# Expert layer 2 of a mixture-of-experts block as seven half-size products, with the experts written out

## The chip, the cores and the metric

One Trainium2 chip, one of its cores. The metric is the device time of one execution in microseconds; lower is better. All data are float32 (some small tables of the first stage are bfloat16).

## The reference, cut to what matters

The program is a block of three layers over 4 images of 32x32 tokens of 384 channels: a selective scan with a depthwise convolution, a linear attention, and a mixture of experts. Only the last is touched:

```python
B, S, D = x.shape                                # 4, 1024, 384
E = router_w.shape[1]                            # 8 experts
T = B * S                                        # 4096 tokens
C = T // E                                       # 512 slots for each expert
...
expert_inputs = jnp.einsum('td,tec->ecd', xf, dispatch)
h = gelu(jnp.einsum('ecd,edm->ecm', expert_inputs, w1) + b1[:, None, :])
expert_outputs = gelu(jnp.einsum('ecm,emd->ecd', h, w2) + b2[:, None, :])
out = jnp.einsum('ecd,tec->td', expert_outputs, combine)
```

For each of the 8 experts, layer 1 takes 512 slots x 384 to 512 x 1536, and layer 2 takes that back to 512 x 384. The gated result is added to the token rows.

## The kernel before

Each engine runs a stream of its own, written by hand, and the streams meet in semaphores. The stages follow each other: the scan (to about 1410 us), its output projection, the attention with the routing (to about 1720 us), and then the experts (to the end).

Before the experts, each token's row has been stored to slot_in in DRAM by its slot, and the token rows to tok_dram and out. An expert e then goes like this; its buffers go by its parity, s.

SyncE (lines 543 to 558) loads w1[s], w2[s] (2.3 MB each) and the slot rows xe. After the first two experts, the loads for e + 2 wait for og_ok, the last gelu of expert e, and all go out together.

TensorE (`turn_slots` from 1474, `expert` from 1481) does three things.
- It transposes xe with 12 instructions into PSUM banks 0 to 2 (line 1478). This is done for e + 1 in the middle of layer 2 of e (TURN_AT = 1, after token tile 1).
- Layer 1 (line 1489): 12 groups m of 128 hidden channels, each of three products (k = 128 channels) over 512 slots, in PSUM banks 3 to 5. From the fourth group on it waits for the gelu of the group three before.
- Layer 2 (line 1502): 4 tiles of 128 slots, each of 12 products over 384 output channels, with the hidden values h_sb as weights and w2 as the moving operand, in banks 6 and 7. It waits for hg_ok of the last gelus at the first tile, and for ob_ok (bank read) at the others.

Each product of float32 operands is two matmul records in the profile, each with a weight load. The program's order on each engine is fixed.

ScalarE (from line 1028) copies the transposed slots to xeT (1032), does the gelu of layer 1 from PSUM to h_sb (1041), and the gelu of layer 2 (1048). VectorE (`owners`, then `expert`) adds the bias b2 to layer 2's PSUM bank into y_pre (2066), and multiplies the gelu by the gate and adds the residual rows (2071). GpSimd (`residuals` 661, `rows_out` 668) gathers residual rows and scatters output rows with indirect DMAs, one of each for a tile of 128 slots; the output rows of e come before the residual rows of e + 1.

Experts 0 to 5 are three turns of a loop over two experts on SyncE, TensorE and VectorE; ScalarE loops over experts 2 to 5. The last two are written out.

Lines of other stages that the prediction reads: 1399 (the attention's 128x128 products, one after the other), 1361 (the transposes behind them), 604 and 587 (GpSimd's products in the scan), 627 and 637 (GpSimd's sums in the two stages after it), 1631, 1856, 1921 and 1963 (VectorE's sums with both inputs in SBUF), 1688 (VectorE's product with an input in PSUM), 531 (the store of token rows to out), 537 (the load of w2[0]).

Of the kernel before, what the change touches and what calls it, by code (L numbers as in the profile page):

```python
# [16 lines left out]
P = 128  # L17
# [39 lines left out]
TURN_AT = 1  # L57
# [101 lines left out]
def hybrid_block_kernel(nc, a, out):  # L159
    with ExitStack() as ctx:  # L160
        def sem(name):
            return ctx.enter_context(nc.semaphore(name))
# [114 lines left out]
        b2_bc = r6y.take(E, C)  # L277
        r6 = Region(arena, R4 + CT * M, COLS)
        w2[0] = r6.take(MT, C)
        xe, xeT, h_sb = r6.take(CPT, CW), r6.take(2, CT, CAP), r6.take(MT, CAP)  # L280
        y_pre, yo, res = r6.take(2, C), r6.take(CPT, C), r6.take(CPT, C)
# [28 lines left out]
        def attend_bank(i):  # L310
            return 4 + (i + 2) % 4


# [3 lines left out]
        token_ok = sem("token_numbers")  # L317
# [5 lines left out]
        cpe_ok, slot_out = sem("conv_filled"), sem("conv_out_of_slot")  # L323
# [30 lines left out]
        tln_ok, x2c_ok, x2_ok = sem("token_var_log"), sem("x2_centred"), sem("x2_ready")  # L354
# [4 lines left out]
            "slots_turned", "slots_turned_copied", "h_filled", "h_gelu", "o_filled", "o_biased", "o_gelu", "rows_scattered"))  # L359
        meta_ok, res_ld, fin_ok = sem("slot_owner"), sem("residuals_in"), sem("final_ready")  # L360
# [19 lines left out]
        def _(sp):  # L380
# [155 lines left out]
            sp.dma_start(xe, slot_in_v[0]).then_inc(ld_xe, 16)  # L536
            sp.dma_start(w2[0], w2_v[0]).then_inc(ld_w2[0], 16)
# [24 lines left out]
        def _(pool):  # L562
# [4 lines left out]
            nc.gpsimd.iota(token, [[P, NT]], base=0, channel_multiplier=1).then_inc(token_ok, 1)  # L567
# [114 lines left out]
        def _(act):  # L682
# [282 lines left out]
            def last_token_std(g):  # L965
                half = slice(4 * g, 4 * g + 4)
                act.wait_ge(tvar_ok, NP + (B - 1) * 2 + (g + 1))
                nc.scalar.activation(rstd5[:, half, 0], mv5[:, half, 1], ACT.Ln, bias=eps_col).then_inc(tln_ok, 1)
                act.wait_ge(tln_ok, g + 1)
                nc.scalar.activation(rstd5[:, half, 0], rstd5[:, half, 0], ACT.Exp, scale=-0.5).then_inc(tstd_ok, 1)  # L970
# [63 lines left out]
            def expert(e, s, first, last):  # L1034
                for m in range(MT):
                    act.wait_ge(h_ok, e * MT + (m + 1))
                    if m == 0:

                        act.wait_ge(o_ok, e * CPT + 2)
                    settled(act)  # L1040
                    nc.scalar.activation(h_sb[:, m], ps[:, 3 + m % 3, :], ACT.Gelu_apprx_tanh,  # L1041
                                         bias=b1_col[:, e, m:m + 1]).then_inc(hg_ok, 1)

                if not first:
                    act.wait_ge(yo_st, e * (16 * CPT))
                for i in range(CPT):
                    act.wait_ge(ob_ok, 1 + e * CPT + (i + 1))
                    nc.scalar.activation(yo[:, i], y_pre[:, i % 2], ACT.Gelu_apprx_tanh).then_inc(og_ok, 1)  # L1048
                    if i == TURN_AT and not last:
                        slots_turned(e + 1, 1 - s)  # L1050

            slots_turned(0, 0)
            expert(0, 0, True, False)
            expert(1, 1, False, False)
            with nc.scalar.Fori(1, E // 2 - 1) as g:
                for s in range(2):
                    expert(g * 2 + s, s, False, False)
            expert(E - 2, 0, False, False)
            expert(E - 1, 1, False, True)
# [3 lines left out]
        def _(pe):  # L1063

            pe.sem_inc(ya_ok, HRING)
            for s in (tp_ok, gr_ok, o_ok):
                pe.sem_inc(s, 2)
# [413 lines left out]
            def expert(e, s, loads, last):  # L1481
                pe.wait_ge(ld_w1[s], loads)
                for m in range(MT):
                    if m >= 3:
                        pe.wait_ge(hg_ok, e * MT + (m - 2))
                    for t in range(CT):
                        if m == 0:
                            pe.wait_ge(xtc_ok, e * CT + (t + 1))
                        mm = pe.matmul(ps[:, 3 + m % 3, :], w1[s][:, t, m * P:(m + 1) * P], xeT[:, s, t],  # L1489
                                       start=(t == 0), stop=(t == CT - 1))  # L1490
                    mm.then_inc(h_ok, 1)
                pe.wait_ge(ld_w2[s], loads)
                for i in range(CPT):
                    if i >= 2:
                        pe.wait_ge(ob_ok, 1 + e * CPT + (i - 1))
                    else:
                        pe.wait_ge(ob_ok, 1 + e * CPT)
                    for m in range(MT):
# [6 lines left out]
                    if i == TURN_AT and not last:  # L1505
                        turn_slots(e + 1)

            turn_slots(0)
            with nc.tensor.Fori(0, E // 2 - 1) as g:
                for s in range(2):  # L1510
                    expert(g * 2 + s, s, g * 16 + 16, False)
            expert(E - 2, 0, 8 * E, False)
            expert(E - 1, 1, 8 * E, True)


        @block.vector
        def _(dve):
# [460 lines left out]
            dve.wait_ge(token_ok, 1)  # L1978
# [79 lines left out]
            def expert(e, s, last):  # L2058
                for i in range(CPT):
                    dve.wait_ge(o_ok, e * CPT + (i + 3))  # L2060

                    if i >= 2:
                        dve.wait_ge(og_ok, 1 + e * CPT + (i - 1))
                    else:
                        dve.wait_ge(og_ok, 1 + e * CPT)
                    nc.vector.tensor_tensor(y_pre[:, i % 2], ps[:, 6 + i % 2, 0:C],  # L2066
                                            b2_bc[:, e, :], ALU.add).then_inc(ob_ok, 1)
                    dve.wait_ge(og_ok, 1 + e * CPT + (i + 1))
                    dve.wait_ge(meta_ok, e + 1)
                    dve.wait_ge(res_ld, e * (16 * CPT) + 16 * CPT)  # L2070
                    nc.vector.scalar_tensor_tensor(out=yo[:, i], in0=yo[:, i], scalar=g_slot[:, s, i:i + 1], in1=res[:, i],  # L2071
                                                   op0=ALU.mult, op1=ALU.add).then_inc(fin_ok, 1)
                    if i == TURN_AT and not last:
                        owners(e + 1, 1 - s)
# [3 lines left out]
            with nc.vector.Fori(0, E // 2 - 1) as g:  # L2078
                for s in range(2):
                    expert(g * 2 + s, s, False)  # L2080
            expert(E - 2, 0, False)
            expert(E - 1, 1, True)


# [79 lines left out]
```

## Time and profile before

| | us |
|---|---|
| median of three runs | 2246.8 (2243.82 to 2249.24) |
| span of the profiled execution | 2244.7 |
| TensorE busy | 1984.1 (88%) |
| VectorE busy | 1575.2 (70%) |
| GpSimd busy | 1297.0 (58%) |
| ScalarE busy | 1144.9 (51%) |

The page gives no time beside the profiled execution's span; the span runs from its first to its last instruction. In the page's slices each digit stands for 1/40 of the span (56.1 us) and is the busy share in tenths. In the chain of waits each piece has its start, its length and what ran. In groups of instructions the columns are line, engine, operation, shapes and count, then busy time and mean ns of one, then idle time before them and what ended it. PE is TensorE, PEld its weight loads, DVE VectorE, ACT ScalarE, POOL GpSimd, SPq the queue that SyncE issues to.

### The profile page before, as it was taken

The numbers are of one execution on the slowest core, as the hardware profiler recorded it, in microseconds if no ns is written. First come the engines' busy times: TensorE is split into PE (matmuls) and PEld (weight loads), VectorE is DVE, ScalarE is ACT, GpSimd is POOL, SyncE is SP. The second block draws the span as 40 slices with busy tenths as digits, with TensorE's granted clock in tenths as the row PEclk, the third lists the DMA queues.
The fourth block names the chain that finished last, engine by engine and source line by source line (L and its number), as shares of the span: only waits on it lengthen the run. The fifth ranks groups of instructions, "written<-read, shape, count | busy, mean of one in ns | idle before, by whom it ended". The sixth has DMA issues, their size and how long they took to land.

```text
span 2244.7 us, 20167 instructions
## 1 busy us (share of the span) xinstructions
PE 1984.1 (88%) x5826; PEld 919.6 (41%) x5830; DVE 1575.2 (70%) x1505; ACT 1144.9 (51%) x1258; POOL 1297.0 (58%) x464
## 2 busy tenths in 40 slices
PE   7988588888888888888888888989995999999997
PEld 3332133333333333333333333456653555555554
DVE  6978999999999999999999999774553000000000
ACT  4788666666776676776767666211213112122111
POOL 0110499999999999999999999401233011111110
PEclk9987599999999999999999999999997999999999
DMA  6448622233222233222232220611226233333300
GB/s 193 151 175 280 212 75 75 70 98 79 84 66 65 75 100 91 65 75 75 61 105 67 77 73 19 229 42 57 85 85 223 85 119 124 123 119 126 126 24 7
DMA packets 82402, 229.13 MB, mean 102 GB/s; under 512 B 14031, under 2 KB 40257, under 8 KB 80816
## 3 DMA queue, kind: packets, MB, share of 16 engines
q1 hardware_dynamic: 76208, 211.54, 29.6%
q0 software_dynamic: 6144, 16.98, 2.1%
q8 instruction: 24, 0.39, 0.1%
q14 instruction: 26, 0.21, 0.0%
HBM read 166.39 MB, written 64.03 MB: 103 GB/s over the span
## 4 chain that ended last, share of the span: by engine, by line
PE 46%; DVE 23%; issue 17%; POOL 8%; ACT 3%; DMA 1%; DVEq 0%; SPq 0%; ACTq 0%; POOLq 0%
DVE arena L1705 15%; PE ps L1489 11%; PE ps L1502 11%; PE ps L1229 6%; POOL arena L604 4%; POOL arena L587 4%; PE ps L1439 3%; PE ps L1213 2%; PE ps L1110 2%; DVE ps L1688 1%; PE ps L1226 1%; PE ps L1139 1%; PE ps L1390 1%; PE ps L1428 1%; DVE arena L1572 1%
## 5 line engine op out<-in xcount | busy, mean ns | idle before, releaser
L604 POOL TENSOR_TENSOR arena<-arena 128x2048 f32<-128x2048 f32 x192 | 868.3, 4533 | 16.6 <-DVE arena L1705 15.7
L1229 PE MATMUL ps<-arena 128*128 128x512 f32 x1536 | 727.7, 596 | 27.7 <-POOL arena L604 27.6
L1705 DVE TENSOR_TENSOR_SCAN arena<-arena,ps 128x1024 f32<-128x1024 f32 x264 | 587.5, 2266 | 0.0
L880 ACT ACTIVATE arena<-ps 128x1024 f32<-128x1024 f32 x384 | 390.7, 1017 | 248.0 <-PE ps L1213 246.1
L1213 PE MATMUL ps<-arena 96*128 (+1 forms) x1296 | 366.7, 384 | 129.3 <-DVE arena L1705 112.7
L1229 PEld LDWEIGHTS ps<-arena 128*128 128x128 f32 x1536 | 288.4, 190 | 287.7 <-issue 194.0
L587 POOL TENSOR_TENSOR arena<-arena 128x1024 f32<-128x1024 f32 x120 | 283.1, 2359 | 103.5 <-DMA arena<-b_rows 103.5
L2066 DVE TENSOR_TENSOR arena<-ps,arena 128x384 f32<-128x384 f32 x32 | 17.8, 557 | 450.4 <-PE ps L1502 450.4
L1688 DVE TENSOR_TENSOR ps<-ps,arena 128x1024 f32<-128x1024 f32 x264 | 309.1, 1216 | 12.6 <-PE ps L1213 12.6
L873 ACT ACTIVATE arena<-arena 128x1024 f32<-128x1024 f32 x264 | 300.8, 1139 | 8.9 <-DVE arena L1705 8.3
L1213 PEld LDWEIGHTS ps<-arena 96*128 96x128 bf16 x1296 | 112.9, 98 | 461.3 <-DVE arena L1705 215.7
L668 POOL DMA_INDIRECT out<-arena x32 | 31.7, 992 | 437.4 <-DVE arena L2071 437.4
L1705 DVE TENSOR_TENSOR_SCAN arena<-ps,arena 128x1024 f32<-128x1024 f32 x120 | 271.5, 2262 | 4.6 <-ACT ps L873 4.2
L1489 PE MATMUL ps<-arena 128*128 128x512 f32 x576 | 250.2, 595 | 0.0
L1502 PE MATMUL ps<-arena 128*128 128x384 f32 x768 | 250.2, 486 | 0.0
L1502 PEld LDWEIGHTS ps<-arena 128*128 128x128 f32 x768 | 145.4, 190 | 101.5 <-issue 3.8
L873 ACT ACTIVATE ps<-arena 128x1024 f32<-128x1024 f32 x120 | 134.1, 1118 | 88.4 <-DVE arena L1705 88.4
L1489 PEld LDWEIGHTS ps<-arena 128*128 128x128 f32 x576 | 110.1, 191 | 136.8 <-issue 134.4
L1041 ACT ACTIVATE arena<-ps,arena 128x512 f32<-128x512 f32 x96 | 66.0, 688 | 176.0 <-PE ps L1489 175.9
L1048 ACT ACTIVATE arena<-arena 128x384 f32<-128x384 f32 x32 | 16.7, 523 | 232.3 <-DVE arena L2066 232.3
L637 POOL TENSOR_TENSOR arena<-arena 128x384 f32<-128x384 f32 x32 | 27.0, 878 | 185.2 <-DVE arena L1863 185.2
L575 POOL COPY arena<-arena 128x1024 f32<-128x1024 f32 x6 | 13.0, 2192 | 134.2 <-ACT arena L729 134.2
(225 smaller groups left out, 1611.9 us busy)
## 6 DMA issues: line engine op xcount, KB each, us to landing
arena<-b_rows SPq DMA_DIRECT2D x240, 256.0 KB, 4.2
arena<-in_w SPq DMA_DIRECT2D x16, 2304.0 KB, 13.3
delta<-arena SPq DMA_DIRECT2D x24, 512.0 KB, 2.9
delta_x<-arena SPq DMA_DIRECT2D x24, 512.0 KB, 3.1
arena<-delta SPq DMA_DIRECT2D x24, 512.0 KB, 3.6
arena<-delta_x SPq DMA_DIRECT2D x24, 512.0 KB, 4.6
slot_in<-arena SPq DMA_DIRECT2D x8, 772.0 KB, 8.1
arena<-slot_in SPq DMA_DIRECT2D x8, 772.0 KB, 18.0
```

What stands on the lines that cost most here:

```text
L587: nc.gpsimd.tensor_tensor(xin[:, x % XRING], xin[:, x % XRING], dux[:, dr], ALU.mult).then_inc(in_ok, 1)
L604: nc.gpsimd.tensor_tensor(hst[:, h:h + 2], hst[:, h:h + 2], c_sb[:, c:c + 2], ALU.mult).then_inc(p2_ok, 2)
L873: nc.scalar.activation(dst, dlt[:, dr], ACT.Exp, scale=a_neg[:, q % OJ, dr, n:n + 1]).then_inc(dec_ok, 1)
L880: nc.scalar.activation(c_sb[:, u % RING], C_PS, ACT.Copy).then_inc(c_free, 1)
L1041: nc.scalar.activation(h_sb[:, m], ps[:, 3 + m % 3, :], ACT.Gelu_apprx_tanh, bias=b1_col[:, e, m:m + 1]).then_inc(hg_ok, 1)
L1213: mm = pe.matmul(dst[:, h * 512:(h + 1) * 512], sel_lhs[0:BR, n], bc[0:BR, q % OJ // J, dr, m, h * 512:(h + 1) * 512], start=True, stop=True)
L1229: mm = pe.matmul(Y_PS[:, h * 512:(h + 1) * 512], ident, hst[:, u % HRING, h * 512:(h + 1) * 512], start=False, stop=(u == UN - 1))
L1439: mm = pe.matmul(ps[:, attend_bank(i), 0:CA], xnT[:, b % 2, t, i * P:(i + 1) * P], w_eff[:, t], start=(t == 0), stop=(t == CT - 1))
L1489: mm = pe.matmul(ps[:, 3 + m % 3, :], w1[s][:, t, m * P:(m + 1) * P], xeT[:, s, t], start=(t == 0), stop=(t == CT - 1))
L1502: mm = pe.matmul(ps[:, 6 + i % 2, 0:C], h_sb[:, m, i * P:(i + 1) * P], w2[s][:, m], start=(m == 0), stop=(m == MT - 1))
L1688: nc.vector.tensor_tensor(x, x, dux[:, dr], ALU.mult).then_inc(p1_ok, 1)
L1705: nc.vector.tensor_tensor_scan(h, f, x, 0.0, ALU.mult, ALU.add).then_inc(sc_ok, 1)
```

## The change

Layer 2 of an expert, a (512 x 1536) by (1536 x 384) product, is split in halves of each side: tokens (TH = 256), hidden channels (KH = 6 tiles of 128) and output channels (CH = 192). Instead of eight half-size products there are seven, by Strassen's scheme in a form of few sums:
- GpSimd forms, for each expert, from the loaded w2: w2_top = b11 + b12, w2_low = b21 + b22, w2_diag = b11 + b22, and in place b12 - b22 and b21 - b11, each over 6 x 192 = 1152 columns. It does so for e + 1 after product M7 of expert e, ahead of that expert's output rows.
- VectorE forms, for each of 6 pairs of hidden tiles, two sums (h_far_near 256 columns, h_both 512) and two differences in place (256 each).
- TensorE's seven products have 6 k tiles x 2 row halves x 192 columns each, in the order M3, M4, M1, (transposes for e + 1), M6, M7, M5, M2, in banks 4 to 7. M7 adds to M1's bank, M5 to M3's, M2 to M4's.
- ScalarE copies M3, M4 and M1 out of PSUM before those banks are added to (s3, s4, s1). VectorE combines these with the banks and the bias, writes yo by halves of the tokens, and ScalarE does the gelu in place on yo.
- Layer 1 takes its 12 groups in the order 0, 6, 1, 7, ... through 4 banks (0 to 3).
- w2[0] and the new buffers lie where the token rows were, so SyncE loads w2[0] only after the stores of these, and VectorE waits for them too. SyncE loads w1 for e + 2 at the end of layer 1 of e, then xe, and w2 at the end of layer 2.
- All experts are written out on all engines. Three semaphores are merged with others (token_ok, tln_ok; slot_out was unused).

```diff
+            def combine_w2(e):
+                w = w2[e % 2]
+                b11, b12, b21, b22 = w[:, 0:KH, 0:CH], w[:, 0:KH, CH:C], w[:, KH:MT, 0:CH], w[:, KH:MT, CH:C]
+                pool.wait_ge(ld_w2[e % 2], 16 * (e // 2 + 1))
+                if e:
+                    pool.wait_ge(o_ok, (e - 1) * PRODUCTS + M7)
+                nc.gpsimd.tensor_tensor(w2_top, b11, b12, ALU.add)
+                nc.gpsimd.tensor_tensor(w2_low, b21, b22, ALU.add)
+                nc.gpsimd.tensor_tensor(w2_diag, b11, b22, ALU.add).then_inc(r_ok, 1)
+                pool.wait_ge(r_ok, 3 * e + 1)
+                nc.gpsimd.tensor_tensor(b12, b12, b22, ALU.subtract).then_inc(r_ok, 1)
+                nc.gpsimd.tensor_tensor(b21, b21, b11, ALU.subtract).then_inc(r_ok, 1)
...
             residuals(0, 0)
+            combine_w2(0)
             for e in range(E):
+                if e + 1 < E:
+                    combine_w2(e + 1)
                 rows_out(e, e % 2)
...
-                    for m in range(MT):
-                        if i == 0 and m in (0, MT - 2, MT - 1):
-
-                            pe.wait_ge(hg_ok, e * MT + max(m + 1, MT - 2))
-                        mm = pe.matmul(ps[:, 6 + i % 2, 0:C], h_sb[:, m, i * P:(i + 1) * P], w2[s][:, m],
-                                       start=(m == 0), stop=(m == MT - 1))
+
+                def product(bank, tokens, weights, fresh, ready):
+                    for k in range(KH):
+                        ready(k)
+                        for r in range(2):
+                            mm = pe.matmul(quarter(bank)[:, r], tokens[:, k, r * P:(r + 1) * P], weights[:, k],
+                                           start=(fresh and k == 0 and r == 0), stop=(k == KH - 1), skip_group_check=True)
                     mm.then_inc(o_ok, 1)
...
+                product(C_PS2, a11, w[:, 0:KH, CH:C], True, near_ready)
+                product(D_PS, a22, w[:, KH:MT, 0:CH], True, far_ready)
+                product(A_PS, h_far_near, w2_diag, True, combined)
+                if e + 1 < E:
+                    turn_slots(e + 1)
+                product(B_PS2, a21_less, w2_top, True, lessened)
+                product(A_PS, a12_less, w2_low, False, kept(3))
+                product(C_PS2, h_both[:, :, 0:TH], w[:, KH:MT, CH:C], False, kept(1))
+                product(D_PS, h_both[:, :, TH:CAP], w[:, 0:KH, 0:CH], False, kept(2))
...
+                for k in range(KH):
+                    dve.wait_ge(hg_ok, e * MT + 2 * k + 2)
+                    near, far = h_sb[:, k], h_sb[:, KH + k]
+                    nc.vector.tensor_tensor(h_far_near[:, k], near[:, 0:TH], far[:, TH:CAP], ALU.add)
+                    nc.vector.tensor_tensor(h_both[:, k], near, far, ALU.add).then_inc(q_ok, 1)
+                    dve.wait_ge(q_ok, 2 * (e * KH + k) + 1)
+                    nc.vector.tensor_tensor(near[:, TH:CAP], near[:, TH:CAP], near[:, 0:TH], ALU.subtract)
+                    nc.vector.tensor_tensor(far[:, 0:TH], far[:, 0:TH], far[:, TH:CAP], ALU.subtract).then_inc(q_ok, 1)
...
+                dve.wait_ge(o_ok, e * PRODUCTS + M5)
+                nc.vector.tensor_tensor(yo[:, 0:2, 0:CH], to_11, quarter(C_PS2), ALU.subtract)
+                nc.vector.tensor_tensor(yo[:, 0:2, CH:C], quarter(C_PS2), bias(1), ALU.add).then_inc(ob_ok, 1)
+                finish(0)
+                dve.wait_ge(o_ok, e * PRODUCTS + M2)
+                nc.vector.tensor_tensor(yo[:, 2:4, CH:C], to_22, quarter(D_PS), ALU.subtract)
+                nc.vector.tensor_tensor(yo[:, 2:4, 0:CH], quarter(D_PS), bias(0), ALU.add).then_inc(ob_ok, 1)
+                finish(1)
...
-            with nc.sync.Fori(0, E // 2 - 1) as g:
-                for s in range(2):
-                    e = g * 2 + s
-
-                    sp.wait_ge(og_ok, 1 + e * CPT + CPT)
-                    sp.dma_start(w1[s], w1_v[g * 2 + (s + 2)]).then_inc(ld_w1[s], 16)
-                    sp.dma_start(w2[s], w2_v[g * 2 + (s + 2)]).then_inc(ld_w2[s], 16)
-                    slots_in(g * 2 + (s + 2))
+            for e in range(E - 2):
+                sp.wait_ge(h_ok, (e + 1) * MT)
+                sp.dma_start(w1[e % 2], w1_v[e + 2]).then_inc(ld_w1[e % 2], 16)
+                slots_in(e + 2)
+                sp.wait_ge(o_ok, (e + 1) * PRODUCTS)
+                sp.dma_start(w2[e % 2], w2_v[e + 2]).then_inc(ld_w2[e % 2], 16)
```

`finish(half)` is the multiply-add of line 2071 for the half's two tiles of 128 slots.

## Rows read from the trace of the kernel before

**Rows 1.** The page: span, and busy tenths and granted clock in 40 slices.
```profile
span 2244.7 us, 20167 instructions
...
PE   7988588888888888888888888989995999999997
...
POOL 0110499999999999999999999401233011111110
PEclk9987599999999999999999999999997999999999
```

**Rows 2.** The chain that ended last, from 1720 us: start, length, what ran.
```profile
1727.22 32.53 PE ps L1489 x72
1759.75 15.48 PE ps L1502 x48
1775.23 1.31 PE ps L1478 x12
...
1792.03 30.90 PE ps L1489 x72
...
2232.96 0.57 DVE arena L2066
...
2233.55 0.53 ACT arena L1048
...
2234.11 0.63 DVE arena L2071
```

**Rows 3.** Groups of instructions, whole run: layer 2's matmuls and their loads.
```profile
L1502 PE MATMUL ps<-arena 128*128 128x384 f32 x768 | 250.2, 486 | 0.0
L1502 PEld LDWEIGHTS ps<-arena 128*128 128x128 f32 x768 | 145.4, 190 | 101.5 <-issue 3.8
```

**Rows 4.** Timeline of TensorE in the attention, 1514.9 to 1517.4: start, length.
```profile
1514.99 2.17 PE L1399 MATMUL ps<-arena 128*128 128x128 f32 x18
1517.00 0.49 PE L1361 MATMUL ps<-arena 128*128 128x128 f32 x3
```

**Rows 5.** Line 1399's weight loads: least, median and most ns.
```profile
L1399 PEld LDWEIGHTS ps<-arena x72: 186/192/193, 1514.9 to 1670.9; 128*128 128x128 f32 x72
```

**Rows 6.** Group of ScalarE in the expert stage: layer 1's gelus.
```profile
L1041 ACT ACTIVATE arena<-ps,arena 128x512 f32<-128x512 f32 x96 | 66.0, 688 | 176.0 <-PE ps L1489 175.9
```

**Rows 7.** Groups of VectorE's sums with both inputs in SBUF.
```profile
L1631 DVE TENSOR_TENSOR arena<-arena 128x1024 f32<-128x1024 f32 x24 | 29.4, 1225 | 0.8
...
L1856 DVE TENSOR_TENSOR arena<-arena 128x384 f32<-128x384 f32 x4 | 2.2, 559 | 0.1
...
L1921 DVE TENSOR_TENSOR arena<-arena 128x64 f32<-128x64 f32 x3 | 0.7, 226 | 0.1
```

**Rows 8.** Groups of GpSimd's two-input instructions.
```profile
L604 POOL TENSOR_TENSOR arena<-arena 128x2048 f32<-128x2048 f32 x192 | 868.3, 4533 | 16.6 <-DVE arena L1705 15.7
...
L627 POOL TENSOR_TENSOR arena<-arena 128x512 f32<-128x512 f32 x9 | 15.1, 1705 | 17.1 <-DVE arena L1746 17.1
```

**Rows 9.** Timeline of GpSimd and VectorE, 1576 to 1580.
```profile
1576.37 6.82 POOL L637 TENSOR_TENSOR arena<-arena 128x384 f32<-128x384 f32 x8 [44.53 <-DVE arena L1863]
...
1578.28 0.84 DVE L1963 TENSOR_TENSOR arena<-arena 128x64 f32<-128x64 f32 x1
```

**Rows 10.** Line 1688, VectorE's product with an input in PSUM: least, median, most ns.
```profile
L1688 DVE TENSOR_TENSOR ps<-ps,arena x264: 1202/1219/1233, 253.5 to 1403.5; 128x1024 f32<-128x1024 f32 x132
```

**Rows 11.** Timeline of SyncE's queue and GpSimd, 1702 to 1729.
```profile
1702.26 0.58 SPq L531 DMA_DIRECT2D out<-arena  x1
...
1720.28 0.51 SPq L537 DMA_DIRECT2D arena<-in_w  x1
...
1728.19 1.00 POOL L661 DMA_INDIRECT arena<-tokens,arena  x1 [0.31 <-issue]
```

**Rows 12.** Lines 531 and 537, in that order: time from issue to landing.
```profile
DMA to landing us min/median/max: 9.6/10.3/11.4
...
DMA to landing us min/median/max: 10.3/10.3/10.3
```

More of the change, by code:

```diff
@@ L56 @@
 CA = CL + E
-TURN_AT = 1
+KH = MT // 2
+TH = CAP // 2
+CH = C // 2
+M3, M4, M1, M6, M7, M5, M2 = range(1, 8)
+PRODUCTS = 7
+UP_BANKS = 4
 class Count:
@@ L277, in hybrid_block_kernel @@
         b2_bc = r6y.take(E, C)
+        r6t = Region(arena, XY, R4)
+        w2[0] = r6t.take(MT, C)
+        h_far_near, h_both = r6t.take(KH, TH), r6t.take(KH, CAP)
+        s3, s4, s1 = (r6t.take(2, CH) for _ in range(3))
+        to_11, to_22 = r6t.take(2, CH), r6t.take(2, CH)
         r6 = Region(arena, R4 + CT * M, COLS)
-        w2[0] = r6.take(MT, C)
+        w2_diag, w2_top, w2_low = (r6.take(KH, CH) for _ in range(3))
         xe, xeT, h_sb = r6.take(CPT, CW), r6.take(2, CT, CAP), r6.take(MT, CAP)
-        y_pre, yo, res = r6.take(2, C), r6.take(CPT, C), r6.take(CPT, C)
+        yo, res = r6.take(CPT, C), r6.take(CPT, C)
         to_row, from_row = r6.take(2, CPT, dtype=U32), r6.take(2, CPT, dtype=U32)
@@ L311, in attend_bank, with quarter @@
             return 4 + (i + 2) % 4
+        def quarter(b):
+            return ps[:, b, 0:2 * CH].rearrange("p (r c) -> p r c", r=2)
+        A_PS, B_PS2, C_PS2, D_PS = 4, 5, 6, 7
+        UP_ORDER = [half * KH + k for k in range(KH) for half in range(2)]
         ld_c, ld_gn, ld_in = sem("ld_consts"), sem("ld_group_sums"), sem("ld_w_in")
@@ L1032, in slots_turned, with expert @@
                     nc.scalar.activation(xeT[:, s, t], ps[:, t, :], ACT.Copy).then_inc(xtc_ok, 1)
-            def expert(e, s, first, last):
-                for m in range(MT):
[L1036 to L1041, printed above, removed]
-                                         bias=b1_col[:, e, m:m + 1]).then_inc(hg_ok, 1)
[L1044 to L1050, printed above, removed]
-            slots_turned(0, 0)
[L1053 to L1059, printed above, removed]
+            def expert(e, s):
+                for n, m in enumerate(UP_ORDER):
+                    act.wait_ge(h_ok, e * MT + (n + 1))
+                    nc.scalar.activation(h_sb[:, m], ps[:, n % UP_BANKS, :], ACT.Gelu_apprx_tanh,
+                                         bias=b1_col[:, e, m:m + 1]).then_inc(hg_ok, 1)
+                for product, kept, bank in ((M3, s3, C_PS2), (M4, s4, D_PS), (M1, s1, A_PS)):
+                    act.wait_ge(o_ok, e * PRODUCTS + product)
+                    nc.scalar.activation(kept, quarter(bank), ACT.Copy).then_inc(s_ok, 1)
+                if e + 1 < E:
+                    slots_turned(e + 1, 1 - s)
+                for half in range(2):
+                    act.wait_ge(ob_ok, 1 + e * 2 + (half + 1))
+                    for i in range(2 * half, 2 * half + 2):
+                        nc.scalar.activation(yo[:, i], yo[:, i], ACT.Gelu_apprx_tanh).then_inc(og_ok, 1)
+            slots_turned(0, 0)
+            for e in range(E):
+                expert(e, e % 2)
         @block.tensor
@@ L1065, in _ @@
             pe.sem_inc(ya_ok, HRING)
-            for s in (tp_ok, gr_ok, o_ok):
+            for s in (tp_ok, gr_ok):
                 pe.sem_inc(s, 2)
@@ L1479, in turn_slots, with expert @@
                     mm.then_inc(xt_ok, 1)
-            def expert(e, s, loads, last):
+            def expert(e, s):
+                w = w2[s]
+                loads = 16 * (e // 2 + 1)
                 pe.wait_ge(ld_w1[s], loads)
-                for m in range(MT):
-                    if m >= 3:
-                        pe.wait_ge(hg_ok, e * MT + (m - 2))
+                for n, m in enumerate(UP_ORDER):
+                    if n >= UP_BANKS:
+                        pe.wait_ge(hg_ok, e * MT + (n - UP_BANKS + 1))
@@ new lines, in lessened, with near_ready, far_ready, combined @@
+                def lessened(k):
+                    pe.wait_ge(q_ok, 2 * (e * KH + k) + 2)
+                def near_ready(k):
+                    if k == 0:
+                        pe.wait_ge(r_ok, 3 * (e + 1))
+                    if e and k == 0:
+                        pe.wait_ge(ob_ok, 1 + 2 * e)
+                    pe.wait_ge(hg_ok, e * MT + 2 * k + 1)
+                def far_ready(k):
+                    pe.wait_ge(hg_ok, e * MT + 2 * k + 2)
+                def combined(k):
+                    pe.wait_ge(q_ok, 2 * (e * KH + k) + 1)
@@ L1516, in _ @@
+                if e + 1 < E:
+                    turn_slots(e + 1)
[3 more added lines that the diff above has]
+                product(D_PS, h_both[:, :, TH:CAP], w[:, 0:KH, 0:CH], False, kept(2))
+            turn_slots(0)
+            for e in range(E):
+                expert(e, e % 2)
         @block.vector
@@ L2056, in owners, with expert, bias, finish @@
                 nc.vector.tensor_copy(g_slot[:, s], xe[:, :, C + 1]).then_inc(meta_ok, 1)
[L2058 to L2074, printed above, removed]
+            def expert(e, s):
+                for k in range(KH):
[6 more added lines that the diff above has]
+                    nc.vector.tensor_tensor(far[:, 0:TH], far[:, 0:TH], far[:, TH:CAP], ALU.subtract).then_inc(q_ok, 1)
+                if e:
+                    dve.wait_ge(yo_st, e * (16 * CPT))
+                if e + 1 < E:
+                    owners(e + 1, 1 - s)
+                def bias(half):
+                    return b2_bc[:, e, half * CH:(half + 1) * CH].unsqueeze(1).to_broadcast([P, 2, CH])
+                dve.wait_ge(s_ok, 3 * e + 2)
+                chain.link(nc.vector.tensor_tensor(s3, s3, s4, ALU.add))
+                nc.vector.tensor_tensor(to_11, s3, bias(0), ALU.add)
+                chain.link(nc.vector.tensor_tensor(to_22, s3, bias(1), ALU.add))
+                dve.wait_ge(s_ok, 3 * e + 3)
+                chain.link(nc.vector.tensor_tensor(to_22, to_22, s1, ALU.add))
+                dve.wait_ge(o_ok, e * PRODUCTS + M6)
+                nc.vector.tensor_tensor(to_22, to_22, quarter(B_PS2), ALU.add)
+                dve.wait_ge(o_ok, e * PRODUCTS + M7)
+                chain.link(nc.vector.tensor_tensor(to_11, to_11, quarter(A_PS), ALU.add))
+                def finish(half):
+                    dve.wait_ge(res_ld, (e + 1) * (16 * CPT))
+                    for i in range(2 * half, 2 * half + 2):
+                        dve.wait_ge(og_ok, 1 + e * CPT + (i + 1))
+                        nc.vector.scalar_tensor_tensor(out=yo[:, i], in0=yo[:, i], scalar=g_slot[:, s, i:i + 1], in1=res[:, i],
+                                                       op0=ALU.mult, op1=ALU.add).then_inc(fin_ok, 1)
+                dve.wait_ge(o_ok, e * PRODUCTS + M5)
[6 more added lines that the diff above has]
+                finish(1)
@@ L2076, in _ @@
             owners(0, 0)
             dve.wait_ge(ld_b2, 16)
[L2078 to L2082, printed above, removed]
+            dve.wait_ge(tok_st, 16 * B)
+            dve.wait_ge(out_st, 16 * B)
+            for e in range(E):
+                expert(e, e % 2)
 def _layouts(i):
```

41 lines of the change are left out of this document (18 added, 23 removed).

## The prediction

> **What bounds the kernel now.** I read first the page's slices, to see which engine is full where. The change touches only the expert stage, the last 520 us. There TensorE is at 9 tenths in every slice, its granted clock is 1.0 after the start, and GpSimd is at 1 tenth [rows 1]. Second the chain of waits from 1720 us on: it is one unbroken file of matmuls. Per expert: layer 1 in 30.90 us for 72 instructions (32.53 in expert 0, which starts at the lower clock), 48 instructions of layer 2 in 15.48, 12 transposes in 1.31, and 48 more of layer 2 in 15.48 [rows 2]. That is 63.17 us, with no waiting in it. So this stage is bound by TensorE; time can be won only by fewer or shorter matmul instructions, or lost by making TensorE wait. Third the groups, for what an instruction costs. One fp32 product is two records. Layer 2 has 768 = 8 experts x 96, 384 columns each [rows 3].
>
> The pitch matters, not the recorded duration (486 ns with its modelled end). It is 15.48/48 = 322.5 ns at 384 columns and 30.90/72 = 429.2 ns at 512. The slope is 106.7/128 = 0.833 ns per column and the rest is 2.5 ns.
>
> **Layer 2 on TensorE.** Per expert the change removes 96 instructions of 384 columns, 30.96 us. It adds 7 products x 6 k tiles x 2 row halves x 2 records = 168 instructions of 192 columns. By the line above, one costs 322.5 - 192 x 0.833 = 162.5 ns; together 27.30 us. Saved: 3.66 us per expert, 29.3 us for eight.
>
> The doubtful point is that 168 weight loads stand where 96 stood, and one load is recorded at 190 ns [rows 3], longer than 162.5. If loads followed each other only end to end, they would set the pitch. The nearest row says that they do not: the 18 matmuls of L1399 are 128 columns wide, each with its own 128x128 load of 186 to 193 ns, and the next line's first matmul starts 2.01 us after the first of them [rows 4, 5]. That is 111.7 ns each, so loads overlap one another. The line gives 109.2 for 128 columns, so the excess is 2.5 ns. With it on all 168 the sum is 27.72 us, 3.4 us dearer over the stage. Bounds for the pitch are therefore 162.5 and 165, and 190 as a rival's. I take 162.5: 192 columns leave a load 50 ns more than the row that already keeps up.
>
> Here a page speaks against the change. The Trainium skill, "TensorE: Matmul & The Clock Gate", Part 3, The mechanism, says that a weight load overlaps matmuls in flight only when it addresses another row group; all loads here fill all rows. By it nothing of a load would be hidden. The trace disagrees: 96 matmuls of 384 columns with 96 loads take 30.96 us [rows 2, 3], which leaves no room for 96 x 190 ns.
>
> **Waits on TensorE.** A wait per k tile is new in the first four products, with the three last 27 waited steps in layer 2 where there were few. Met waits cost nothing in the trace: layer 1 has a wait at each group of 6 and still fits the line. So the question is whether each is met. I count t from the end of layer 1's matmuls. The products run M3 at 0 to 3.9, M4 to 7.8, M1 to 11.7, transposes to 13.0, M6 to 16.9, M7 to 20.8, M5 to 24.7, M2 to 28.6.
> - M3 and M4 need gelus only. A group of layer 1 takes 2.58 us and a gelu 0.69 [rows 6]; the last is done at about 0.9, and M4's last k tile needs it at about 7.
> - M1 and M6 need VectorE's sums. Per k these are three of 256 and one of 512 columns, with two SBUF inputs. From 1225 ns at 1024 columns and 559 at 384 [rows 7] the slope is 1.04 ns, so 426 and 692 ns: 1.97 us per k, against 5.15 us between pairs of gelus. The last sums end at 0.9 + 2.0 = 2.9; M1 starts at 7.8. Hidden, with 4.9 us to spare. Six k cost VectorE 12 us of an engine that was idle.
> - M7, M5 and M2 need ScalarE's three copies, each under that gelu's 0.69 us [rows 6], being narrower; the latest must be done between 11.7 and 16.9. Hidden.
> - M3 needs GpSimd's five weight sums of 1152 columns. GpSimd's plain rate is 4533/2048 = 2.21 ns per column, its slowest 1705/512 = 3.33 [rows 8]: 12.7 to 19.2 us. For the next expert they start when M7 ends (20.8) and are wanted when the next layer 1 ends (59.5): 38.7 us. Hidden; at under three times the plain rate they would be late. Behind them on GpSimd are queued the output rows of this expert and the residual rows of the next, eight issues of 1.3 us (1.00 and the 0.31 ahead of it [rows 11]); VectorE asks for these only late in the next layer 1 and in its layer 2.
>
> **GpSimd against VectorE.** While GpSimd adds, VectorE's instructions with two SBUF inputs are held. A 64-column sum takes 0.84 us beside GpSimd's eight adds of 0.85 us each, against 0.226 alone [rows 7, 9]; the ones with an input in PSUM keep to 1202 to 1233 ns in a stage where GpSimd is 9 tenths busy [rows 1, 10]. So about one held instruction gets through per GpSimd instruction. In the 12.7 us after M7 that hits two residual multiply-adds of the first half: some 2 x 2.6 us instead of 1.2. M5 ends at 24.7, the two PSUM sums at 25.9, the gelus at 27.0, the multiply-adds at 32.2, the second half's sums at 33.4 and its gelus at 34.5. These gelus stand before the next layer 1's on ScalarE, whose first was due at 31.2 and now comes at 35.2. TensorE wants it only at its fifth group, 28.6 + 10.3 = 38.9, since there are four banks. Hidden, with 3.7 us.
>
> **Loads and SyncE.** w2[0] is now behind a wait for the token stores. These were issued by 1702.3 and land in at most 11.4 us; w2[0] was issued at 1720.3 and landed after 10.3, at 1730.6 [rows 11, 12]. So the wait is met, GpSimd's first sums end by 1744 to 1750, and layer 1 ends at 1759.75. The steady loads move: w1 goes out at the end of layer 1, w2 at the end of layer 2, each more than 40 us before use. Writing the experts out removes branches that cost nothing: the chain shows no gap between experts. The fetching of more code has no row of its own; I take nothing, as for the attention's straight code, whose matmuls follow each other without a gap [rows 4], and leave it to the third rival's price as the upper end.
>
> **The end.** After the last matmul the chain is 0.57, 0.53 and 0.63 us, then GpSimd's issue [rows 2]. Now two sums come first and two rows are finished together: sums 1.14, gelu 0.53, multiply-adds 1.26, 2.93 against 1.73, +1.2 us. Two GpSimd issues follow at 1.3 us [rows 11] where one stood alone; the first starts a multiply-add earlier, so +0.6. Together +1.8 us.
>
> **Sum.** 8 x 3.66 = 29.3, less 1.8: 27.5 us off. The profiled span 2244.7 becomes 2217.2. The median is 2246.8, 2.1 above that span, so 2219.3.
>
> **Rivals.**
> - Loads set the pitch, at 190 ns. Layer 2 takes 168 x 0.190 = 31.9 us, 0.96 more than now; eight times that and the end's 1.8 give +9.5: 2256.3. For it: the recorded load. Against: L1399. The change turns into a loss from a pitch of 183 ns on (8 x 168 x 0.183 + 1.8 = 8 x 30.96). Chance 0.05, of which 0.01 is for no overlap at all: 168 x (190 + 160) ns = 58.8 us per expert, near 2471, the outcome of the page's rule.
> - GpSimd starves VectorE wholly at its slowest rate. The sums after M7 end at 40.0; only then come the second multiply-add, two PSUM sums and three gelus, to 43.5. TensorE stands 4.6 us seven times, 32 us: 2251. TensorE begins to stand once GpSimd's run ends later than 35.4, and the change is a loss from 39.3 on (27.5/7 = 3.9 us later). For it: the held sums. Against: one got through per GpSimd instruction. Chance 0.04.
> - Part of the gain goes: a short bubble where a product or k tile starts. If at each of the 42 k steps, waited or not, one load shows what it exceeds a matmul by, 190 - 162.5 = 28 ns, that is 1.2 us per expert, 9.3 us: 2228.6. Against: met waits cost layer 1 nothing. Code fetch would land in the same place. Chance 0.10.
> - The gain is all there: 0.79, with 2215 to 2225 as its own range (the pitch's 3.4 us above, the median's own scatter of 2.7 below and above).
> - The remainder, 0.02, is no change, by several small losses.
>
> **Numbers.** Time 2219.3. The range leaves out the slower rivals only: 2214.5 to 2230. About 0.2% (4.5 us) is what a measurement can tell from no change. Faster 0.88, same 0.03, slower 0.09.
>
> **What would show it.** Right: layer 2's records at a pitch of 162 to 165 ns, 27.3 us of products per expert, no TensorE idle time between 1727 and the end, a stage of 59.5 us per expert. The pitch at 190 shows the first rival. Idle time before the fifth group of layer 1, released by ScalarE, shows the second; idle time at M3 would mean GpSimd's sums are late, at M1 VectorE's. A forecast that fails with all waits met fails on the pitch.

## The result and the profile after

The changed kernel takes 2217.64 us (median of four runs, 2216.44 to 2220.36) against 2245.85 (four runs, 2243.82 to 2249.24): 28.2 us less, a ratio of 0.9876 (95% interval 0.9865 to 0.9888). The profiled execution's span is 2215.2 us, 29.5 less than before's 2244.7. The forecast was 27.5 us less.

The page of after: the span, the busy tenths and the granted clock in 40 slices.

```profile
span 2215.2 us, 21161 instructions
...
PE   7987588888888888888888888889996899999997
...
DVE  6988999999999999999999999783556343443332
...
POOL 0110399999999999999999999701223344444430
PEclk9987599999999999999999999999999999999999
```

Against [rows 1], TensorE is about as full in the last ten slices as it was, and from the 32nd slice to the last but one GpSimd and VectorE are now at 3 to 4 tenths. The bound has not moved. The chain that ended last, from 1720 us (start, length, what ran), shows the same file of matmuls as [rows 2], shorter:

```profile
1726.84 30.95 PE ps L1514 x72
1757.79 11.70 PE ps L1522 x72
1769.49 1.31 PE ps L1501 x12
1770.80 15.60 PE ps L1522 x96
1786.40 30.90 PE ps L1514 x72
...
2174.38 27.32 PE ps L1522 x168
2201.71 0.56 DVE arena L2147
2202.27 0.48 DVE arena L2148
2202.77 0.53 ACT arena L1078
2203.39 0.62 DVE arena L2139
```

Layer 1 is L1514, layer 2 is L1522. The 72 + 96 instructions of layer 2 take 27.30 us, 162.5 ns each. One expert takes 30.90 + 11.70 + 1.31 + 15.60 = 59.51 us against 63.17, and no piece of another engine stands between the first matmul and 2201.7.

The groups of after in the expert stage (busy us, mean ns, idle us before and its releaser), which answer to [rows 3]:

```profile
L1522 PE MATMUL ps<-arena 128*128 128x192 f32 x1344 | 220.9, 326 | 0.0
L1522 PEld LDWEIGHTS ps<-arena 128*128 128x128 f32 x1344 | 218.7, 190 | 3.8 <-issue 3.8
```

1344 loads of 190 ns would be 255 us end to end; they fit in 218.7, so they overlap one another. The matmul's recorded 326 ns is as far above its pitch as before's 486 was.

Where the 29.5 us of span went, piece by piece:

| piece | before | after | difference |
|---|---|---|---|
| start of expert 0's layer 1 | 1727.22 | 1726.84 | -0.4 |
| expert 0's layer 1 | 32.53 | 30.95 | -1.6 |
| from there to the last matmul's end | 473.2 | 443.9 | -29.3 |
| from there to the end of the span | 11.7 | 13.5 | +1.8 |

### The profile page after: what moved, and what is told of

Read it like the earlier page. It is cut to its first block, busy times and chain, and to the rows that moved or that the text cites. A ratio compares the mean times of both kernels' runs of the same rounds, so it can differ in the third digit from the quotient of the medians.

```text
span 2215.2 us, 21161 instructions
## 1 busy us (share of the span) xinstructions
PE 1951.5 (88%) x6402; PEld 990.9 (45%) x6406; DVE 1725.4 (78%) x1745; ACT 1153.6 (52%) x1282; POOL 1409.9 (64%) x504
## 4 chain that ended last, share of the span: by engine, by line
PE 45%; DVE 23%; issue 17%; POOL 8%; ACT 3%; DMA 1%; DVEq 1%; SPq 0%; ACTq 0%; POOLq 0%
DVE arena L1754 15%; PE ps L1514 11%; PE ps L1522 10%; PE ps L1252 7%; POOL arena L619 4%; POOL arena L602 4%; PE ps L1462 3%; PE ps L1236 2%; PE ps L1133 2%; DVE ps L1737 1%; PE ps L1249 1%; PE ps L1413 1%; PE ps L1451 1%; PE ps L1162 1%; DVE arena L1621 1%
## 5 line engine op out<-in xcount | busy, mean ns | idle before, releaser
L1252 PE MATMUL ps<-arena 128*128 128x512 f32 x1536 | 727.9, 596 | 27.6 <-POOL arena L619 27.5
L1252 PEld LDWEIGHTS ps<-arena 128*128 128x128 f32 x1536 | 288.4, 190 | 287.9 <-issue 194.3
L1514 PE MATMUL ps<-arena 128*128 128x512 f32 x576 | 248.6, 592 | 0.0
L1522 PE MATMUL ps<-arena 128*128 128x192 f32 x1344 | 220.9, 326 | 0.0
L1522 PEld LDWEIGHTS ps<-arena 128*128 128x128 f32 x1344 | 218.7, 190 | 3.8 <-issue 3.8
L693 POOL TENSOR_TENSOR arena<-arena 128x1152 f32<-128x1152 f32 x8 | 20.9, 2618 | 244.6 <-PE ps L1522 244.4
L1514 PEld LDWEIGHTS ps<-arena 128*128 128x128 f32 x576 | 109.4, 190 | 133.9 <-issue 133.9
L2111 DVE TENSOR_TENSOR arena<-arena 128x256 f32<-128x256 f32 x48 | 20.4, 424 | 128.4 <-ACT arena L1068 117.4
```

The source lines that it names most:

```text
L1252: mm = pe.matmul(Y_PS[:, h * 512:(h + 1) * 512], ident, hst[:, u % HRING, h * 512:(h + 1) * 512], start=False, stop=(u == UN - 1))
L1514: mm = pe.matmul(ps[:, n % UP_BANKS, :], w1[s][:, t, m * P:(m + 1) * P], xeT[:, s, t], start=(t == 0), stop=(t == CT - 1))
L1522: mm = pe.matmul(quarter(bank)[:, r], tokens[:, k, r * P:(r + 1) * P], weights[:, k], start=(fresh and k == 0 and r == 0), stop=(k == KH - ...
```

## The experiments

All run on one core of a chip beside the kernel before. Layer 1 of expert 0, whose code is nearly the same in all of them, takes between 30.9 and 32.6 us in their profiles, by the moment at which the granted clock rises, and it ends between 1757.4 and 1760.1 us. Spans can therefore be compared to some 2.8 us, pieces of the chain much closer.

**The experts written out, nothing else.** In the kernel before:

```diff
-            with nc.tensor.Fori(0, E // 2 - 1) as g:
+            for g in range(E // 2 - 1):
```
and the same on SyncE, ScalarE and VectorE.

> The kernel before, with only the expert loops of all engines written out. Theory: the branches and the fetching of code cost nothing either way; the same time within 0.1%, 63.17 us per expert in the chain. Rival, writing out wins or loses something at each of the loop turns: over 0.2 us beside each expert's 63.17.

Measured: 2244.88 us, ratio to before 0.9994 (0.9984 to 1.0003). The starts of layer 1 in the chain are 63.17 us apart, as in [rows 2]:

```profile
1790.56 30.90 PE ps L1489 x72
...
1853.73 30.90 PE ps L1489 x72
```

Writing out costs and brings nothing that can be seen; the whole gain is that of the products.

**Eight half-size products instead of seven.** In the kernel before, each 384-column product as two of 192:

```diff
-                        mm = pe.matmul(ps[:, 6 + i % 2, 0:C], h_sb[:, m, i * P:(i + 1) * P], w2[s][:, m],
-                                       start=(m == 0), stop=(m == MT - 1))
+                        for lo in (0, C // 2):
+                            mm = pe.matmul(ps[:, 6 + i % 2, lo:lo + C // 2], h_sb[:, m, i * P:(i + 1) * P], w2[s][:, m, lo:lo + C // 2],
+                                           start=(m == 0 and lo == 0), stop=(m == MT - 1), skip_group_check=True)
```

> The kernel before, with each 384-column product of layer 2 done as two of 192 columns: 192 loads and matmuls per expert, eight half-size products' worth. Theory: only the 2.5 ns per instruction is added, 192 x 162.5 = 31.20 us against 30.96 per expert, +1.9 us in all (0.1%). Rival, the loads set the pitch at 190 ns: 36.5 us per expert, +44 us.

Measured: 2246.38 us, ratio 1.0007 (0.9997 to 1.0016). In the chain, the last expert's layer 2, without the transposes between:

```profile
2170.71 30.90 PE ps L1489 x72
2201.61 31.21 PE ps L1503 x192
```

31.21/192 = 162.6 ns. Twice the loads cost 0.25 us per expert, the 2.5 ns per instruction. That load time does not set the pitch at 192 columns is shown here without any other part of the change. Seven against eight is then 31.2 to 27.3.

**How narrow can a product be?** In the changed kernel each product takes a width of its own.

```diff
+WIDTH = {1: 192, 2: 160, 3: 128, 4: 96, 5: 64, 6: 48, 7: 32}
...
-                            mm = pe.matmul(quarter(bank)[:, r], tokens[:, k, r * P:(r + 1) * P], weights[:, k],
+                            mm = pe.matmul(quarter(bank)[:, r, 0:wd], tokens[:, k, r * P:(r + 1) * P], weights[:, k, 0:wd],
```

> The changed kernel, but its seven products move only 192, 160, 128, 96, 64, 48 and 32 columns (in the order M3, M4, M1, M6, M7, M5, M2) instead of 192 each; it leaves out the rest of layer 2's output columns. Theory: loads overlap one another, so the pitch follows 2.5 + 0.833 ns per column (162.5, 135.8, 109.2 ns) down to a floor set by the loads; from line 1399 of before (111.7 ns at 128 columns, 2.5 above the line) I expect that floor near 110 ns, so M6, M7, M5 and M2 all at about 110, layer 2 in 24 x (162.5 + 135.8 + 111.7 + 4 x 110) = 20.4 us per expert, 2218 - 8 x 6.9 = 2163 us. Rival, loads one after the other at their recorded 190 ns: every product at 190, 31.9 us per expert, slower than now. Rival, no floor: 14.8 us per expert, 2118 us.

Measured: 2186.2 us in a single run, 23 more than expected. The chain of one expert where the clock held in layer 2, and the next layer 1:

```profile
1816.23 9.84 PE ps L1524 x72
1826.07 1.31 PE ps L1502 x12
1827.38 10.64 PE ps L1524 x96
1838.02 32.68 PE ps L1515 x72
```

The first three products (192, 160, 128 columns) make 9.84/24 us = 410 ns together; less 162.5 and 135.8 that leaves 111.7 ns for 128 columns, as for line 1399 in [rows 4]. The last four (96, 64, 48, 32) take 10.64/96 = 110.8 ns, where their widths would ask for 52.5 on average. So the floor was forecast right, and both rivals fall. What was not forecast is the layer 1 behind them, 32.68 us instead of 30.90. The windows of this kernel (stretch, its length, busy time of PE, PEld, DVE, ACT and POOL, then the granted clock, DMA share and GB/s):

```profile
1777.00:1780.00 3.00, 3.00 (x30) 3.00 (x28) 0.82 (x3) 0.00 (x0) 3.00 (x2) 1.00 0.00 0
1780.00:1783.25 3.25, 3.25 (x19) 3.25 (x19) 2.58 (x3) 0.94 (x2) 3.25 (x2) 0.55 0.00 0
1783.25:1786.50 3.25, 3.25 (x5) 1.30 (x5) 2.92 (x3) 0.30 (x1) 3.17 (x2) 0.50 0.64 155
1786.50:1816.23 29.73, 29.73 (x71) 13.26 (x69) 13.16 (x22) 8.20 (x13) 12.27 (x10) 0.99 0.33 113
```

TensorE's records fill the whole of each stretch, and still its granted clock went from 1.0 (2.4 GHz) to 0.5 (1.2 GHz) while M2, the 32-column product, ran (from 1779.1 us here), and was back 3.9 us into layer 1. The trace has such a fall in seven of the eight experts: in five of them while M2 ran, in two within 0.5 us behind it, and in none under the 96-, 64- or 48-column products. Behind six of seven experts the next layer 1 then took 32.4 to 33.9 us instead of 30.9. Where the clock fell early in M2 the last 96 instructions took up to 12.77 us instead of 10.64, so the lower clock lengthens the floor too: M2 took some 4.8 us there instead of 2.7. Together these come to 21 of the 23 us; the other 2 lie ahead of the change, where layer 1 of expert 0 starts 2.4 us later than in after (1729.21 against 1726.84). The Trainium skill, "TensorE: Matmul & The Clock Gate", Terms, describes the gate as one that follows how busy the engine is. The record does not show what set it off: it is full throughout, but a matmul's recorded end is modelled (a 48-column one is recorded at 275 ns where they follow each other every 111), so it could not show gaps between them.

**All products at 128 or at 96 columns.** To see whether the clock falls at any product near the floor:

```diff
+WIDTH = {n: 128 for n in range(1, 8)}
```
and 96 in the other.

> The changed kernel with all seven products moving 128 columns instead of 192; it leaves out a third of layer 2's output columns. Theory, the floor of the loads is at 110.8 ns: 168 x 111.7 = 18.8 us of products per expert at full clock, 51.0 us per expert, 2218 - 8 x 8.5 = 2150 us, if the granted clock stays at 1.0. In the run with mixed widths it fell to 0.5 behind the narrow products; whether it falls here too is open, and each fall would cost some 2 us of an expert.

> The same with 96 columns; it leaves out half of layer 2's output columns. Theory, a floor at 110.8 ns: 18.6 us of products per expert, no faster than at 128 columns, or slower if the granted clock falls more often. Rival, no floor: 168 x 82.5 = 13.9 us per expert, 38 us less than at 128 columns.

Measured: 2148.93 us and 2148.77 us, one run each. The chains of one expert, at 128 columns and then at 96:

```profile
1828.40 30.90 PE ps L1515 x72
1859.30 8.04 PE ps L1524 x72
...
1868.65 10.72 PE ps L1524 x96
```
```profile
1828.46 30.93 PE ps L1515 x72
1859.39 8.01 PE ps L1524 x72
...
1868.71 10.69 PE ps L1524 x96
```

That is 111.7 and 111.3 ns. At 96 columns a product with its own load is no shorter than at 128, and in both kernels the granted clock was 1.00 from 1777 us to the last matmul. So neither the pitch of 111 ns nor products of 96 columns alone brought the fall; no kernel has 64, 48 or 32 columns throughout, so which of these the fall needs stays open. The Trainium skill, "TensorE: Matmul & The Clock Gate", LDWEIGHTS, gives a load's time as its columns over 1.2 GHz, an estimate of 107 ns for 128 columns; the floor measured here at full clock is 4 to 5 ns above that.

**The weight sums on VectorE.** The five sums move from GpSimd to VectorE, behind each expert's second half.

```diff
-                nc.gpsimd.tensor_tensor(w2_top, b11, b12, ALU.add)
+                nc.vector.tensor_tensor(w2_top, b11, b12, ALU.add)
...
             for e in range(E):
                 expert(e, e % 2)
+                if e + 1 < E:
+                    combine_w2(e + 1)
```

> The changed kernel with the weight sums on VectorE, after each expert's second half, instead of GpSimd. Theory: GpSimd's hold on VectorE is real but hidden, so the two multiply-adds of the first half fall from 5.5 us to 1.2 and the time stays at that of the changed kernel within 0.1%; five sums of 1152 columns take VectorE about 1.36 us each, 6.8 us, inside the next layer 1. Rival, the contention costs the changed kernel time somewhere: this one is faster by over 2 us.

Measured: 2216.73 us, ratio to before 0.9871 (0.9855 to 0.9888), against 2217.64 and 0.9876 for the changed kernel: the same. The contention itself is plain. First the timeline of after at the end of layer 2 of expert 1 (TensorE's layer 1 of expert 2 starts at 1845.9), then this kernel's at the same place:

```profile
1843.44 2.62 POOL L695 TENSOR_TENSOR arena<-arena 128x1152 f32<-128x1152 f32 x1
1843.80 5.56 DVE L2139 SCALAR_TENSOR_TENSOR arena<-arena 128x384 f32<-128x384 f32 x2 [0.66 <-ACT arena L1078]
...
1846.14 2.81 POOL L697 TENSOR_TENSOR arena<-arena 128x1152 f32<-128x1152 f32 x1
1848.91 2.95 POOL L698 TENSOR_TENSOR arena<-arena 128x1152 f32<-128x1152 f32 x1
1849.29 0.54 DVE L2147 TENSOR_TENSOR arena<-arena,ps 128x384 f32<-128x384 f32 x1
...
1851.17 1.25 ACT L1068 ACTIVATE arena<-ps,arena 128x512 f32<-128x512 f32 x2
```
```profile
1843.37 1.15 DVE L2123 SCALAR_TENSOR_TENSOR arena<-arena 128x384 f32<-128x384 f32 x2 [0.66 <-ACT arena L1062]
1845.52 0.56 DVE L2131 TENSOR_TENSOR arena<-arena,ps 128x384 f32<-128x384 f32 x1 [1.00 <-PE ps L1506]
```

Two multiply-adds take 5.56 us beside GpSimd's sums and 1.15 without. Each ends 0.4 us behind the end of one of GpSimd's instructions (1846.06 and 1848.95), and GpSimd's own grow from 2.62 to 2.81 and 2.95. The sum with an input in PSUM (L2147) keeps its 0.54 while GpSimd runs, as forecast from [rows 10]. The sums themselves take VectorE 1.36 us each.

**Two banks for layer 1,** to take away the cover of that delay, which is the time that TensorE can work on before it needs what is late:

```diff
-UP_BANKS = 4
+UP_BANKS = 2
```

> The changed kernel with layer 1 in two PSUM banks instead of four. In the changed kernel's trace layer 1's first gelu ends 5.95 us after layer 1 starts, because it stands behind the second half's gelus, which stand behind the held multiply-adds; with two banks TensorE wants that bank at 5.15. Theory: TensorE stands 0.85 us at the third group of experts 1 to 7, +6 us in all (0.27%), released by ScalarE. Rival, a two-bank ring costs at every group: the gelu needs 0.9 of 2.58 us, so by the trace it doesn't; if it did, 10 groups x 8 experts x some 0.2 us, +16 us or more.

Measured: 2225.37 us, ratio 0.9917 (0.9901 to 0.9934). The chain around the start of expert 2's layer 1:

```profile
1843.96 0.53 ACT arena L1078
...
1844.59 5.55 DVE arena L2139 x2
...
1851.10 0.94 ACT arena L1078 x2
1852.04 0.58 ACT arena L1068
...
1852.67 26.02 PE ps L1514 x60
```

Now the held multiply-adds are on the path: TensorE's third group waits for the first gelu, 0.82 us idle. The same group of expert 1 starts at 1792.07, so the expert's period is 1852.67 - 1792.07 = 60.60 us, 1.09 more than 59.51. Of the 0.27 beyond the idle time 0.17 is the modelled end of the last matmul before it, which hides in an unbroken file; the last 0.1 has no cause that the trace names. Seven times 1.09 is 7.6 us; the span is 7.3 longer than after's. The expectation had the place and the releaser right and the price 1.6 us too low. No other group waits, and the granted clock stays at 1.00.

**Two banks and the weight sums on VectorE.**

> Two banks, and the weight sums on VectorE. Theory: without GpSimd's hold the second half's gelus come about 4.4 us earlier, the first gelu of layer 1 is on time, and the 0.85 us wait is gone: the time of the changed kernel within 0.1%. Rival, the wait of the two-bank kernel has another cause than GpSimd's hold: as slow as the two-bank kernel.

Measured: 2217.12 us, ratio 0.9877 (0.9860 to 0.9893), with no idle time of TensorE from 1727 us on. Taking GpSimd off gives the 8.3 us back. So the two-bank kernel's wait is GpSimd's hold on VectorE, and four banks are what hides it.

**More weight sums on GpSimd.** Five, then ten, more sums of the same size ahead of each expert's five, into a spare buffer:

```diff
+                for n in range(5):
+                    if e or n:
+                        pool.wait_ge(again_ok, e * 5 + n)
+                    nc.gpsimd.tensor_tensor(again, b11, b12, ALU.add).then_inc(again_ok, 1)
```
and 10 for 5 in the second.

> The changed kernel with five more GpSimd sums of 1152 columns ahead of each expert's five (written to a spare buffer). In the changed kernel's trace the five take 13.8 us from the end of M7. Theory: VectorE gets one held instruction through per GpSimd instruction, so the second half's gelus come as early as before and only the deadline of M3 counts: the run of sums ends about 27.4 us after M7, 11 us before M3; no TensorE idle time, the time of the changed kernel within 0.1%. Rival, VectorE is held until GpSimd's run ends: the multiply-add ends 28 us after M7, the next layer 1 waits at its fifth group for about 11 us, seven times, +75 us.

Measured: 2217.70 us, ratio 0.9879 (0.9863 to 0.9896): the time of the changed kernel. In expert 0 TensorE waited 0.4 us for the sums, once; nowhere else. GpSimd's run is 28.1 us here. Had VectorE been held until its end, the next layer 1 would have stood; it got one instruction through per GpSimd instruction instead. Lines of VectorE and GpSimd from this run, the last of them behind GpSimd's run:

```profile
1855.61 2.92 POOL L700 TENSOR_TENSOR arena<-arena 128x1152 f32<-128x1152 f32 x1
1855.98 2.83 DVE L2117 TENSOR_TENSOR arena<-arena 128x256 f32<-128x256 f32 x1
1858.49 2.79 POOL L701 TENSOR_TENSOR arena<-arena 128x1152 f32<-128x1152 f32 x1
1858.73 3.10 DVE L2118 TENSOR_TENSOR arena<-arena 128x512 f32<-128x512 f32 x1
...
1867.28 0.41 DVE L2117 TENSOR_TENSOR arena<-arena 128x256 f32<-128x256 f32 x1
```

> The same with ten more sums. Theory: the run takes 13.8 + 10 x 2.7 = 40.8 us and ends 2.1 us behind the end of the next layer 1 (38.7 us after M7), so M3 waits some 2 to 4 us, seven times, and in expert 0 not at all or little (its sums start 3.5 us into layer 1 and would end 13 us late: +13 once): +27 to +41 us against the changed kernel. Rival, the cover is larger because GpSimd's sums start before M7 ends: no difference.

Measured: 2272.39 us, ratio to before 1.0117 (1.0100 to 1.0134), so 55 us behind the changed kernel, where 27 to 41 were expected. TensorE's timeline (start, length, in brackets the idle time before and its releaser):

```profile
1772.80 14.86 PE L1528 MATMUL ps<-arena 128*128 128x192 f32 x72 [14.39 <-POOL arena L704]
...
1869.54 31.06 PE L1520 MATMUL ps<-arena 128*128 128x512 f32 x72
1904.28 13.65 PE L1528 MATMUL ps<-arena 128*128 128x192 f32 x72 [3.68 <-POOL arena L704]
```

The place and the releaser are as expected: M3 waits for the last sum. The eight waits add up to 40.2 us, the upper end of the range: 14.4 in expert 0 and 3.7 in each of the others, because GpSimd's instructions last 2.7 to 3.1 us beside VectorE's sums. What was left out is the clock. Behind each wait the first three products take 13.65 us instead of 11.86 (14.86 in expert 0), because the granted clock has fallen, 15.5 us in all. Three stretches of this kernel (columns as above), the first of them the wait itself; the clock fell only 1.0 us behind it:

```profile
1835.30:1839.14 3.84, 0.16 (x1) 0.00 (x1) 3.84 (x2) 0.69 (x1) 3.79 (x2) 1.00 0.56 203
1839.14:1842.00 2.86, 2.86 (x12) 2.86 (x13) 2.79 (x7) 0.00 (x0) 2.14 (x3) 0.67 1.03 430
1842.00:1845.00 3.00, 3.00 (x16) 3.00 (x15) 2.96 (x8) 0.00 (x0) 2.39 (x3) 0.74 0.83 333
```

Per expert that makes 65.14 us (1904.28 - 1839.14) against 59.51: 5.6 us for an idle time of 3.7. Seven of these and expert 0's 14.4 + 3.0 are 57 us, which is the difference of the spans (2272.3 and 2215.2).

## Why the prediction was right, point by point

- **The pitch of 162.5 ns.** Right to the last digit: 27.30 us of products per expert, 29.3 us saved over eight. That loads overlap one another, read from line 1399 in [rows 4, 5], was the step on which the forecast rested. The first rival, loads at 190 ns, is shown wrong by the changed kernel itself and by the eight half-size products; no overlap at all, the outcome by the rule on row groups in the Trainium skill, "TensorE: Matmul & The Clock Gate", Part 3, The mechanism, even more so: the trace disagrees with it at 162.5 ns. The upper bound of 165 ns was not needed: the 2.5 ns excess at 128 columns is the floor showing, not a tax on every narrow product.
- **Waits met.** All were: from 1720 us on TensorE's only wait is the one for expert 0's slot rows, ahead of the first transposes. VectorE's last work on h ended 2.6 us after layer 1's end (forecast 2.9), 5.2 before M1. The copies cost 0.49 us each (under 0.69 forecast). The weight sums took 13.6 us (forecast 12.7 to 19.2) of a cover of 38.7. The run with three times the sums shows that this cover is as long as was worked out: at 42.3 us the wait is 3.7. So the sums would be late from 38.7/12.7 = 3.05 times the plain rate on, not from under three times, as the prediction has it.
- **GpSimd against VectorE.** Right in kind and near in size: 5.56 us for the two multiply-adds (forecast 5.2), and layer 1's first gelu ended 5.95 us into layer 1 where TensorE wants it at 10.3. The forecast had 3.7 us to spare; it was 4.3. That this is real cover and not an idle worry is shown by the two-bank pair. The rival of VectorE held until the end of GpSimd's run is shown wrong by the run with twice the sums, and GpSimd's slowest rate, the 3.33 ns per column of [rows 8], was not met either: 2.95 us for 1152 columns is 2.56.
- **Part of the gain lost in bubbles.** Did not happen; the 168 instructions follow each other at 162.5 ns across all 27 waited steps. Written-out code costs nothing, as the kernel before with its experts written out shows.
- **The end.** +1.8 us forecast, +1.8 measured (11.7 to 13.5). Its two parts are near: 1.0 up to the last multiply-add's end (forecast 1.2) and 0.8 behind it (0.6).
- **The sum.** 27.5 us forecast on the span, 29.5 seen. The 2.0 between them lie ahead of the change: 0.4 at the start and 1.6 in expert 0's layer 1, where the clock rose earlier in this execution: it was granted at 0.50 from 1725 to 1728 us and at 0.60 from 1728 to 1731 in before, at 0.70 and 1.00 in after. Variants of the changed kernel show the same spread there (31.75 with the sums on VectorE, 32.57 with two banks too), so it is a scatter of executions and no effect of the change. The medians differ by 28.2, between forecast and span.
- **A reading that was loose.** In [rows 1] TensorE's last slice stands at 7 tenths and not at 9, and a 9 for the granted clock says only 90% or more. The stage is full all the same: the chain of before has no gap, and its granted clock was 1.00 from 1840 to 1850. Nothing in the sum hangs on it.

## What to carry to other kernels

Where TensorE is full and everything else is idle, fewer products bought with additions on the idle engines gave the whole of their count back here, at 192 columns. By the pitches measured this should hold down to 128 columns (111.7 ns); below that, at 96 columns and in the mix of 96 to 32, a matmul record of an fp32 product with its own 128x128 load took 111 ns at full clock whatever its width. A second level of halving here would make 96-column products and would pay that floor. Look up a narrow product in the trace of before and divide its stretch by its count; the recorded duration of a load says nothing of how loads follow each other.

An engine given new work can hold another through the SBUF they share; price the held instructions, and ask which buffer ring hides them. A wait of TensorE of 3.7 us costs 5.6, since the clock falls behind it: cover that ends just short of the need can be dearer than the shortfall. The wait of 0.8 us in the two-bank kernel brought no fall and cost 1.1.

## What was not expected of the hardware

- The granted clock fell to 0.5 behind an unbroken run of 96-, 64- and 48-column products, under the 32-column one or just behind it, in seven of eight experts. In the six of them that are followed by a layer 1 it stayed low for the first 2.7 to 5.6 us of that. With 96 or 128 columns throughout, at the same pitch, it did not fall in the one run of each. What sets it off is left open.
- One VectorE instruction with both inputs in SBUF gets through per GpSimd two-input instruction, however short it is, and GpSimd's own grow by 0.2 to 0.4 us of 2.62 each time. That the two contend over a shared interface is in the Trainium skill, "GPSIMD Engine Reference", Key points, and the trace agrees; what it costs is read from the trace: 2.8 us instead of 0.6 for a multiply-add, 2.8 instead of 0.4 for a 256-column sum.
